# Moving the bias and residual-branch additions of a two-layer metaformer kernel from VectorE to ScalarE and TensorE

## The chip, the cores and the metric

The kernel runs on one core of one Trainium2 chip. The metric is the device time of one execution in microseconds (us), lower is better. An engine is named PE (TensorE, matmuls), DVE (VectorE), ACT (ScalarE), POOL (GpSimd) or SP (SyncE, which only issues transfers here).

## The reference

Input is a batch of 32 images of 96 channels and 48 x 48 pixels. Layer 0 normalises over channels, runs a state-space scan in an order sorted by similarity, adds a local branch (a depthwise convolution, batch normalisation and SiLU), gates and projects the sum, and adds the input back. Then comes a feed-forward layer in emulated low precision. Layer 1 is a 3 x 3 deformable convolution (offsets and masks are predicted from the normalised input, each tap is sampled bilinearly) and a second feed-forward layer. What the change touches, cut down:

```python
out = out_mamba + lc                       # lc: SiLU of the normalised local branch
out = transpose(out) * softmax(z)          # one gate per channel and image
out = out @ out_proj_w.T + out_proj_b      # then x = x + out

def _qlinear(x, W, b):                     # q_mul: 5 exponent, 2 mantissa bits; q_acc: 5 and 10
    y = q_acc(q_mul(x) @ q_mul(W).T)
    return q_acc(y + q_mul(b))
h = relu(_qlinear(_ln_t(t), W1, b1))       # 96 -> 384
t = t + _qlinear(h, W2, b2)                # 384 -> 96
```

## The kernel before

Pass one (from the start to about 10,200 us of the profile) does the scan and leaves the local branch and the scan's result of every image in DRAM. Pass two, which the change touches, does the rest image by image.

Pass two works in periods. An image has NCH = 6 chunks of CH = 384 pixels, and a period handles one chunk of each of several roles at once, for neighbouring images: role c (gate, projection, residual and first feed-forward layer of a chunk), role d (normalisation for layer 1 and the table of corner rows that the sampling reads), role q (offsets and masks), role e (deformable convolution and second feed-forward layer), role f (the second feed-forward layer's last step and the store). A period has 12 steps, numbered u = 0 to 11. In every period the 3 tiles of 128 pixels of role e are sampled: POOL issues 9 indirect gathers for each tile (line 1623, 27 in a period, 162 in an image) into a ring of 4 buffers G, ahead of their use, and may refill a buffer when PE has transposed its tile. DVE multiplies the gathered corners by their weights in `multiply` (lines 1907 to 1912) and adds them in `add_corner` (lines 1925 and 1927), PE transposes the sums (line 1641), ACT copies them to SBUF in `columns` (line 1791).

Each engine runs its instructions strictly in the written order: step by step, and within a step in the order of the code. Semaphores tie the engines together. The order of the work that matters here, for one period, from one deformable convolution to the next:

- u = 3: PE runs the deformable convolution (`convolve`, line 1654, 18 instructions). It waits for ACT's copy of the table rows (`prow`, line 1842).
- u = 3 to 5: first layer normalisation: PE centres (line 1661), ACT squares (1797), PE takes the mean (1668), ACT does Ln (1802) and Exp (1805), DVE multiplies (`xq`, line 1940).
- u = 5 and 6: first linear layer of role c: three matmuls (1678), three copies to 16-bit floats on ACT (`rounded`, line 1812).
- u = 6 and 7: the normalisation of role e in the same manner. At u = 7 DVE adds the bias to the three blocks and takes the positive part (`biased`, line 1948), and ACT turns them to 8-bit floats (`quantized`, line 1819).
- u = 8 and 9: second linear layer (PE, line 1686), copy to 16 bits on ACT (line 1869); DVE adds the second bias (line 1955) and the residual (line 1957, `x_2`). ACT then runs `columns` and the offsets' copy `offc` (line 1852, with a bias).
- u = 10: PE spreads the offsets (line 1756), does the rest of the first linear layer of role e (1678), and centres `x_2` (1661); ACT rounds and squares.
- u = 11: PE takes the mean (1668); DVE runs `biased` for role e; ACT runs `quantized` for role e and then Ln and Exp of the last normalisation, in this order.
- u = 0 (next period): DVE makes `xflat` (line 1975) and adds the local branch to the scan's result (`mix`, line 1980). PE runs the second linear layer of role e (1686), ACT copies it (1832), DVE adds bias and residual at u = 1.
- u = 1 and 2: PE projects (line 1711, one float32 matmul of 384 columns in two instructions) and then transposes `xflat` (line 1721); ACT copies the transposed rows (`prow`, 1842), which frees the next convolution.

Two things happen once in an image. In period 5 (periods of an image are numbered 0 to 5), step 1, and in period 1, step 1, DVE computes sampling positions and weights (`positions`, lines 1550 to 1569). At the end of period 4 ACT applies SiLU to the local branch of the next image but one, between two loads of its function table (line 1881), and DVE's `mix` waits for it.

The 16-bit and 8-bit blocks are `h16`, `r16`, `hq`, `y16`, `z16`; PSUM bank BM takes the projection.

## Time and profile before

| | us |
|---|---|
| runs | 18383.95, 18420.75, 18424.49 |
| median of the runs | 18420.75 |
| span of the profiled execution | 17175.7 |
| median less span | 1245.05 |
| DVE busy in the span | 14514.2 (85%) |
| PE / POOL / ACT busy | 12732.8 (74%) / 12401.2 (72%) / 8968.6 (52%) |

The profile covers the time from the first to the last instruction. The profiled execution's own device time is not listed apart from its span; the three timed runs lie 0.2% from end to end, and what lies around the span is taken as 1245.05 us, the median less the span. Line numbers are those of the kernel before.

### The profile page before, as it was taken

How to read it: one execution, taken by the hardware profiler on the slowest of the kernel's cores; microseconds unless marked ns; L12 is line 12 of the kernel's file. 1: busy time of each engine (PE TensorE's matmuls, PEld its weight loads, DVE VectorE, ACT ScalarE, POOL GpSimd, SP SyncE). 2: the span in 40 equal slices, each digit the busy share in tenths (PEclk: the TensorE clock that was granted, in tenths of full speed). 3: DMA queues.
4: the chain of work that ended last, by engine and by line, in shares of the span. 5: the costliest groups of instructions: out<-in, count | busy, mean ns of one | idle time of the engine just before them, and what ended most of it. 6: DMA issues, size and time to landing. Idle time of an engine off the chain costs nothing. (4 is left out here: it accounts for less than half of the span.)

```text
span 17175.7 us, 183440 instructions
## 1 busy us (share of the span) xinstructions
PE 12732.8 (74%) x51055; PEld 6059.9 (35%) x51055; DVE 14514.2 (85%) x19220; ACT 8968.6 (52%) x16380; POOL 12401.2 (72%) x10756
## 2 busy tenths in 40 slices
PE   6777777777777777777787646777777777777776
PEld 3333333333333333333333312333333333333333
DVE  5888888888888888888888855988898989899998
ACT  4555655656556555565565534444444444444443
POOL 3777777777777777777777744777777777777776
PEclk9999998999999998999999867888888888888887
DMA  2333333333433333333433335666666666666665
GB/s 55 94 97 96 99 100 98 99 95 96 104 94 95 101 98 98 98 98 99 101 97 95 96 90 137 186 187 186 186 188 185 186 192 188 188 188 186 187 188 155
DMA packets 1297936, 2234.90 MB, mean 130 GB/s; under 512 B 713341, under 2 KB 759125, under 8 KB 1284629
## 3 DMA queue, kind: packets, MB, share of 16 engines
q1 hardware_dynamic: 896022, 1090.20, 25.1%
q0 software_dynamic: 368640, 1076.24, 22.3%
q10 hardware_dynamic: 32256, 56.64, 1.1%
q8 instruction: 425, 6.96, 0.2%
q14 instruction: 593, 4.86, 0.1%
HBM read 1493.27 MB, written 275.76 MB: 103 GB/s over the span
## 5 line engine op out<-in xcount | busy, mean ns | idle before, releaser
L1623 POOL DMA_INDIRECT G<-corners,idx x5184 | 4964.2, 958 | 1992.1 <-issue 1554.4
L1383 POOL TENSOR_TENSOR hc<-h,crep 128x768 f32<-128x768 f32 x2304 | 4176.4, 1815 | 2206.5 <-DVE h L1157 1233.9
L1141 DVE TENSOR_TENSOR ps<-dxr,ps 128x768 f32<-128x768 f32 x2304 | 2186.3, 949 | 1041.2 <-PE ps L750 1024.9
L1157 DVE TENSOR_TENSOR_SCAN h<-decay,carry,ps 128x768 f32<-128x768 f32 x1536 | 2776.4, 1808 | 145.5 <-ACT decay L972 85.3
L761 PE MATMUL ps<-hc,sel 128*96 128x512 f32 (+1 forms) x6144 | 2581.8, 548 | 353.4 <-POOL hc L1383 198.7
L972 ACT ACTIVATE decay<-dtr,a_neg 128x768 f32<-128x768 f32 x2304 | 2117.8, 926 | 348.2 <-DVE h L1157 332.8
L750 PE MATMUL ps<-bq,pick 128*128 128x512 bf16 (+1 forms) x4608 | 1233.8, 353 | 991.3 <-DVE h L1157 806.1
L1912 DVE TENSOR_TENSOR G<-G,ps 128x1152 f32<-128x1152 f32 (+1 forms) x1152 | 1724.7, 1497 | 0.0
L761 PEld LDWEIGHTS ps<-hc,sel 128*96 128x96 f32 x6144 | 1022.7, 182 | 1608.1 <-issue 1204.8
L1654 PE MATMUL ps<-cols_t,w_def 128*96 128x384 f32 x3456 | 1342.5, 550 | 178.3 <-ACT prow L1842 172.2
L869 PE MATMUL ps<-xcp,w_local 128*96 128x384 f32 x3456 | 1436.8, 538 | 40.7 <-POOL xcp L1357 39.2
L1925 DVE TENSOR_TENSOR ps<-ps,G 128x384 f32<-128x384 f32 (+1 forms) x2304 | 1407.4, 611 | 47.1
L1157 DVE TENSOR_TENSOR_SCAN h<-decay,ps 128x768 f32<-128x768 f32 x768 | 1342.2, 1748 | 32.3 <-ACT decay L972 2.5
L980 ACT ACTIVATE carry<-h 128x1 f32<-128x1 f32 x1536 | 303.0, 197 | 1934.4 <-DVE h L1157 1932.8
L810 PE MATMUL ps<-xnp,w_conv 128*96 128x384 f32 x3456 | 1292.6, 513 | 24.5 <-ACT x_in L1009 22.3
L1797 ACT ACTIVATE sq<-ps 96x384 f32<-96x384 f32 x576 | 280.1, 486 | 1944.1 <-PE ps L1661 1944.1
L1641 PE MATMUL ps<-ident,G 128*128 128x128 f32 x5184 | 1005.9, 311 | 94.2 <-DVE G L1927 93.1
L750 PEld LDWEIGHTS ps<-bq,pick 128*128 128x128 bf16 x4608 | 377.7, 101 | 1803.2 <-DVE h L1157 923.5
L1791 ACT ACTIVATE cols_t<-ps 128x512 f32<-128x512 f32 (+1 forms) x1728 | 832.8, 483 | 324.2 <-PE ps L1641 323.1
L1641 PEld LDWEIGHTS ps<-ident,G 128*128 128x128 f32 x5184 | 764.0, 162 | 466.6 <-issue 282.9
L1654 PEld LDWEIGHTS ps<-cols_t,w_def 128*96 128x96 f32 x3456 | 626.5, 187 | 831.3 <-issue 598.1
L1686 PE MATMUL ps<-hq,w2q 128*96 128x384 fp8e5 x1152 | 312.0, 389 | 773.8 <-ACT rs L1805 489.4
(243 smaller groups left out, 23803.3 us busy)
## 6 DMA issues: line engine op xcount, KB each, us to landing
crep<-c_rows SPq DMA_DIRECT2D x3072, 96.0 KB
dtr<-rel SPq DMA_DIRECT2D x2304, 96.0 KB, 2.2
dxr<-one_e SPq DMA_DIRECT2D x2304, 96.0 KB
corners<-prow SPq DMA_DIRECT2D x1536, 72.0 KB
G<-corners,idx POOLq DMA_INDIRECT x5184
x_in<-in_x SPq DMA_DIRECT2D x32, 864.0 KB, 6.6
local_all<-local_c ACTq DMA_DIRECT2D x192, 144.0 KB
sim<-sorted_rows SPq DMA_DIRECT2D x32, 864.0 KB, 6.8
```

Of the source, the lines that this page charges most:

```text
L750: m = pe.matmul(wide(bank_of("step", s), P)[:, a:b], Wt["pick"][:, ng, :], M["tall"]["bq"][:, q % 2, a:b], start=True, stop=True)
L761: m = pe.matmul(wide(BY, C)[:, a:b], Wt["sel"][:, cg, :], hc[:, v % HC, a:b], start=(v % ROUND == 0), stop=(v % ROUND == ROUND - 1))
L869: m = pe.matmul(ps[0:C, BV, 0:CH], Wt["w_local"][:, t, :], M["tall"]["xcp"][:, 8 * c + t // 3:8 * c + t // 3 + 8, t % 3:t % 3 + W], start= ...
L972: act.activation(decay[:, s % 3, :], dtr[:, q % 2, cg, :], ACT.Exp, scale=Wt["a_neg"][:, direction(q)[0], ng, cg:cg + 1]).then_inc(S["s_de ...
L1141: dve.tensor_tensor(drive, dxr[:, q % 2, cg, :], drive, ALU.mult).then_inc(S["s_drive"], 1)
L1157: dve.tensor_tensor_scan(along(h[:, v % HR, :], k), along(decay[:, v % 3, :], k), along(wide(bank_of("step", v % STEPS), P), k), first, AL ...
L1383: pool.tensor_tensor(hc[:, v % HC, :], h[:, v % HR, :], crep[:, g % CRING, :], ALU.mult).then_inc(S["s_weighted"], 1)
L1623: pool.indirect_dma_start(M["G"][:, slot(g), k, :], None, table(r), bass.IndirectOffsetOnAxis(M["idx"][side(r)][:, t, k:k + 1], 0)).then_i ...
L1641: m = pe.transpose(ps[:, BT + n % 2, (k % 4) * P:(k % 4 + 1) * P], M["G"][:, slot(t - 1), k, 0:P], ident[:])
L1654: m = pe.matmul(ps[0:C, BN, 0:CH], Wt["w_def"][:, k, :], M["cols"][:, of_e(w)[1] % 2, k, :], start=(k == 0), stop=(k == TAPS - 1))
L1912: dve.tensor_tensor(rows[:, :, 1:], rows[:, :, 1:], by[:, :, 1:].unsqueeze(3).to_broadcast([P, n, CORNERS - 1, C]), ALU.mult).then_inc(S[" ...
L1925: dve.tensor_tensor(acc[:, 0:n], acc[:, 0:n], rows[:, :, q], ALU.add).then_inc(S["p_half"], 1)
```

## The change

Three edits, all in pass two. First, `biased` moves from DVE to ACT: one activation Relu with a per-partition bias for each of the three blocks; the first block is placed at the end of step 6 (role c) or 10 (role e), the other two in step 7 or 11 right ahead of `quantized`. Second, the addition of the second bias moves from DVE to ACT as an Identity activation with a bias, behind the copy of the matmul's result (`returned`); DVE keeps the residual addition. Third, DVE's `mix` is dropped: PE projects the scan's result and the local branch in two matmuls that add up in one PSUM group. SP now loads the next local branch behind the projection (`p_proj`) and no longer behind `mix`. `local_t` gets 128 partitions. Cut to its core:

```diff
--- before.py
+++ after.py
@@ -1422,7 +1422,7 @@
     return dict(
-        tall=tall, x2=[low("x2_0", [L]), low("x2_1", [L])], x_t=low("x_t", [L]), local=b("local_t", [C, L]),
+        tall=tall, x2=[low("x2_0", [L]), low("x2_1", [L])], x_t=low("x_t", [L]), local=low("local_t", [L]),
         mix=low("mix", [L]), wg=low("wg", [C]), xn=low("xn2", [PH, PW]), xflat=b("xflat", [C, CH]),
@@ -1576,10 +1576,8 @@
                     if c is not None:
-                        sp.wait_ge(S["p_mix"], nth(of_c, w) + 1)
+                        sp.wait_ge(S["p_proj"], nth(of_c, w) + 1)
                     sp.dma_start(M["local"][:], dram["local"][image(n)]).then_inc(S["p_local"], 16)
-                    if c is not None:
-                        sp.wait_ge(S["p_proj"], nth(of_c, w) + 1)
                     sp.dma_start(M["mix"][:], dram["mamba"][image(n)]).then_inc(S["p_mamba"], 16)
@@ -1703,13 +1701,16 @@
                 if u == 1 and c is not None:
-                    pe.wait_ge(S["p_mix"], nc_ + 1)
                     if w % NCH == LASTP:
+                        pe.wait_ge(S["p_mamba"], 16 * (next_before(w) + 1))
+                        pe.wait_ge(S["p_silu"], next_before(w) + 1)
                         pe.wait_ge(S["p_gate"], next_before(w) + 1)
...
                         pe.wait_ge(S["p_xn"], nd + 1)
-                    pe.matmul(ps[0:C, BM, 0:CH], M["tall"]["wg"][:], M["tall"]["mix"][:, part(c[1])], start=True,
-                              stop=True).then_inc(S["p_proj"], 1)
+                    for name in ("mix", "local_t"):
+                        m = pe.matmul(ps[0:C, BM, 0:CH], M["tall"]["wg"][:], M["tall"][name][:, part(c[1])],
+                                      start=(name == "mix"), stop=(name == "local_t"))
+                    m.then_inc(S["p_proj"], 1)
                 if u == 1 and d is not None:
@@ -1812,10 +1813,29 @@
 
+            def biased(kind, w, b1, first, last):
+
+                i = turn[kind, w]
+                if first == 0 and turn_before(kind, w):
+                    act.wait_ge(S["p_quant"], NHID * turn_before(kind, w))
+                for j in range(first, last):
+                    act.wait_ge(S["p_rnd"], NHID * i + j + 1)
+                    act.activation(r16[:, KIND[kind], j, :], h16[:, KIND[kind], j, :], ACT.Relu,
+                                   bias=b1[:, j:j + 1]).then_inc(S["p_bias"], 1)
+
+            def returned(n, place, z, b2, done):
+
+                act.wait_ge(S["p_lin" + n], place + 1)
+                act.activation(y16[:, z, :], ps[0:C, BV, 0:CH], ACT.Copy).then_inc(S["p_yr" + n], 1)
+                act.wait_ge(S["p_yr" + n], place + 1)
+                if place:
+                    act.wait_ge(S[done], place)
+                act.activation(z16[:, z, :], y16[:, z, :], ACT.Identity, bias=b2).then_inc(S["p_yb" + n], 1)
+
             def quantized(kind, w):
 
-                act.wait_ge(S["p_bias"], turn[kind, w] + 1)
                 for j in range(NHID):
+                    act.wait_ge(S["p_bias"], NHID * turn[kind, w] + j + 1)
                     act.activation(hq[:, KIND[kind], j, :], r16[:, KIND[kind], j, :], ACT.Copy,
@@ -1828,8 +1848,7 @@
                 if u == 0 and f is not None:
-                    act.wait_ge(S["p_lin3"], nf + 1)
-                    act.activation(y16[:, 1, :], ps[0:C, BV, 0:CH], ACT.Copy).then_inc(S["p_yr3"], 1)
+                    returned("3", nf, 1, Wt["b2q"][1][:], "p_y")
                 if u == 1 and d is not None:
@@ -1847,6 +1866,8 @@
                     rounded("c", w, u - 5)
+                    if u == 6:
+                        biased("c", w, Wt["b1q"][0], 0, 1)
                 if q is not None and u == 9:
@@ -1863,15 +1884,18 @@
                 if u == 7 and c is not None:
+                    biased("c", w, Wt["b1q"][0], 1, NHID)
                     quantized("c", w)
                 if u == 8 and c is not None:
-                    act.wait_ge(S["p_lin1"], nc_ + 1)
-                    act.activation(y16[:, 0, :], ps[0:C, BV, 0:CH], ACT.Copy).then_inc(S["p_yr1"], 1)
+                    returned("1", nc_, 0, Wt["b2q"][0][:], "p_x2")
                 if u in (9, 10) and e is not None:
                     rounded("e", w, u - 9)
+                    if u == 10:
+                        biased("e", w, Wt["b1q"][1], 0, 1)
                 if u == 10 and c is not None:
...
                 if u == 11 and e is not None:
+                    biased("e", w, Wt["b1q"][1], 1, NHID)
                     quantized("e", w)
@@ -1939,21 +1963,9 @@
 
-            def biased(kind, w, b1):
-
-                dve.wait_ge(S["p_rnd"], NHID * (turn[kind, w] + 1))
-                if turn_before(kind, w):
-                    dve.wait_ge(S["p_quant"], NHID * turn_before(kind, w))
-                for j in range(NHID):
-                    m = dve.tensor_scalar(r16[:, KIND[kind], j, :], h16[:, KIND[kind], j, :], b1[:, j:j + 1], 0.0,
-                                          ALU.add, ALU.max)
-                m.then_inc(S["p_bias"], 1)
-
-            def residual(n, c, place, z, b2, res, dst, bsem, done):
-
-                dve.wait_ge(S["p_yr" + n], place + 1)
-                dve.tensor_scalar(z16[:, z, :], y16[:, z, :], b2, None, ALU.add).then_inc(S[bsem], 1)
-                dve.wait_ge(S[bsem], place + 1)
+            def residual(n, c, place, z, res, dst, done):
+
+                dve.wait_ge(S["p_yb" + n], place + 1)
                 dve.tensor_tensor(dst[:, part(c)], res[:, part(c)], z16[:, z, :], ALU.add).then_inc(S[done], 1)
@@ -1973,18 +1985,12 @@
                     dve.tensor_tensor(M["xflat"][:], ps[0:C, BM, 0:CH], M["rs"][:], ALU.mult).then_inc(S["p_xn"], 1)
-                if u == 0 and c is not None:
-                    if p == LASTP:
-                        dve.wait_ge(S["p_silu"], next_before(w) + 1)
-                        dve.wait_ge(S["p_mamba"], 16 * (next_before(w) + 1))
-                    dve.tensor_tensor(M["mix"][:, part(c[1])], M["mix"][:, part(c[1])], M["local"][:, part(c[1])],
-                                      ALU.add).then_inc(S["p_mix"], 1)
                 if p == 1 and u == 1 and has(k):
...
                 if u == 1 and f is not None:
-                    residual("3", f[1], nf, 1, Wt["b2q"][1][:], M["x3"], M["x3"], "p_yb3", "p_y")
+                    residual("3", f[1], nf, 1, M["x3"], M["x3"], "p_y")
                 if u == 2 and c is not None:
@@ -1994,14 +2000,10 @@
                     normalize("1", nc_, BM, M["rs"], M["xq"], "p_xq1", saturate=False)
-                if u == 7 and c is not None:
-                    biased("c", w, Wt["b1q"][0])
                 if u == 8 and e is not None:
...
                 if u == 9 and c is not None:
-                    residual("1", c[1], nc_, 0, Wt["b2q"][0][:], M["x_t"], x2[side(c[0])], "p_yb1", "p_x2")
-                if u == 11 and e is not None:
-                    biased("e", w, Wt["b1q"][1])
+                    residual("1", c[1], nc_, 0, M["x_t"], x2[side(c[0])], "p_x2")
                 if of_tile(t) is not None and sub % 2 == 0:
```

## Rows read from the trace of the kernel before

**Rows 1.** Head of the page: span.
```profile
span 17175.7 us, 183440 instructions
```

**Rows 2.** Stretches: us, then busy us (x) of PE, PEld, DVE, ACT, POOL; clock, DMA, GB/s.
```profile
11370.95:16798.14 5427.19, 3999.02 (x15445) 1984.94 (x15445) 4883.92 (x9127) 2613.97 (x5850) 4033.75 (x4213) 0.81 0.67 187
15358.00:15369.10 11.10, 4.57 (x28) 2.85 (x25) 10.18 (x18) 7.58 (x21) 8.36 (x10) 1.00 0.55 154
15394.60:15406.71 12.11, 7.87 (x22) 4.08 (x22) 11.17 (x21) 6.02 (x14) 9.06 (x11) 0.50 0.69 186
```

**Rows 3.** Groups by line and shape, 12000 to 16000 us.
```profile
L1623 POOL DMA_INDIRECT G<-corners,idx x3104 | 2971.6, 957 | 1028.8 <-issue 931.1 <-PE ps L1641 97.8
...
L1819 ACT ACTIVATE hq<-r 128x384 fp8e5<-128x384 f16 x690 | 308.3, 509 | 251.3 <-DVE r L1948 251.3
...
L1948 DVE TENSOR_SCALAR r<-h,b1q 128x384 f16<-128x384 f16 x690 | 204.2, 350 | 0.0
...
L1711 PE MATMUL ps<-mix,wg 128*96 128x384 f32 x230 | 173.3, 857 | 41.4 <-DVE mix L1980 41.4
...
L1955 DVE TENSOR_SCALAR z<-y,b2q 96x384 f16<-96x384 f16 x230 | 76.8, 334 | 5.2
...
L1852 ACT ACTIVATE offc<-ps,off_bias 96x384 f32<-96x384 f32 x115 | 65.2, 567 | 0.0
...
L1980 DVE TENSOR_TENSOR mix<-mix,local_t 96x384 f32<-96x384 f32 x115 | 62.8, 546 | 56.4 <-ACT local_t L1881 56.4
```

**Rows 4.** Waits, same stretch: who waited for whom, us, times, longest.
```profile
POOL G L1623 <- issue: 931.1, 3056, 0.3
...
ACT hq L1819 <- DVE r L1948: 251.3, 115, 2.9
...
POOL G L1623 <- PE ps L1641: 97.8, 48, 4.9
```

**Rows 5.** Timeline of PE: the deformable convolution of seven periods (start, length).
```profile
15340.68 6.02 PE L1654 MATMUL ps<-cols_t,w_def 128*96 128x384 f32 x18 [0.94 <-ACT prow L1842]
...
15373.67 6.02 PE L1654 MATMUL ps<-cols_t,w_def 128*96 128x384 f32 x18 [0.94 <-ACT prow L1842]
...
15406.71 8.04 PE L1654 MATMUL ps<-cols_t,w_def 128*96 128x384 f32 x18 [0.94 <-ACT prow L1842]
...
15444.18 8.09 PE L1654 MATMUL ps<-cols_t,w_def 128*96 128x384 f32 x18 [0.94 <-ACT prow L1842]
...
15480.75 6.02 PE L1654 MATMUL ps<-cols_t,w_def 128*96 128x384 f32 x18 [0.94 <-ACT prow L1842]
...
15513.64 6.02 PE L1654 MATMUL ps<-cols_t,w_def 128*96 128x384 f32 x18 [0.94 <-ACT prow L1842]
...
15548.94 1.50 PE L1654 MATMUL ps<-cols_t,w_def 128*96 128x384 f32 x4 [0.94 <-ACT prow L1842]
```

**Rows 6.** Timeline of ACT in the first two of those periods.
```profile
15363.50 0.49 ACT L1797 ACTIVATE sq<-ps 96x384 f32<-96x384 f32 x1
15366.71 1.35 ACT L1819 ACTIVATE hq<-r 128x384 fp8e5<-128x384 f16 x3 [2.73 <-DVE r L1948]
...
15389.34 1.33 ACT L1819 ACTIVATE hq<-r 128x384 fp8e5<-128x384 f16 x3
...
15395.90 0.49 ACT L1797 ACTIVATE sq<-ps 96x384 f32<-96x384 f32 x1 [0.73 <-PE ps L1661]
15399.16 1.35 ACT L1819 ACTIVATE hq<-r 128x384 fp8e5<-128x384 f16 x3 [2.77 <-DVE r L1948]
```

**Rows 7.** Timeline of PE in the second of those periods.
```profile
15403.43 1.49 PE L1711 MATMUL ps<-mix,wg 128*96 128x384 f32 x2
15404.71 0.85 PE L1721 MATMUL ps<-ident,xflat 96*96 96x96 f32 x4
```

**Rows 8.** Timeline of DVE: layer 1 normalisation in the second and the fourth period.
```profile
15383.00 0.55 DVE L1940 TENSOR_TENSOR xq<-ps,rs 96x384 fp8e5<-96x384 f32 x1 [1.21 <-ACT rs L1805]
...
15457.88 0.55 DVE L1940 TENSOR_TENSOR xq<-ps,rs 96x384 fp8e5<-96x384 f32 x1
```

2 lines of the change are left out of this document (1 added, 1 removed).

## Prediction

> **What bounds the kernel now.** I read the head of the page first: a span of 17175.7 us [rows 1], so 1245.05 us of the median of 18420.75 lie outside it, and I leave them as they are. The change touches pass two alone, so the next view is the table of stretches over 26 whole images of it [rows 2]: 5427.19 us, or 208.7 us an image and 34.8 a period. DVE is busy for 4883.92 of them (90%), POOL for 74%, ACT for 48%. The reader should distrust both 90% and 74%.
>
> POOL first. In 4000 us it is busy for 2971.6 us and sits for another 931.1 in gaps of 0.3 us with nothing to wait for [rows 3, 4]. So a gather costs 0.957 + 0.300 = 1.257 us of POOL, and the 162 of an image cost 203.7 us. POOL waits for a free buffer for 97.8 us in 19 images, 5.1 us an image [rows 4]. POOL is therefore a floor 5.0 us below today's 208.7, or 33.9 us a period: 32 x 5.0 = 160 us is the most that any relief of the other engines can return.
>
> Then the periods. The timeline of the deformable convolution [rows 5] gives the six intervals of an image, named by the periods at their ends: 2 to 3 32.99, 3 to 4 33.04, 4 to 5 37.47, 5 to 0 36.57, 0 to 1 32.89, 1 to 2 35.30, together 208.26. The convolution takes 6.02 us at the upper level of the clock and 8.04 to 8.09 where it starts at the lower one.
>
> Last, inside a period. ACT waits once in each period for DVE's `biased` of role e, 251.3 us in 115 periods or 2.2 each, and this is its longest wait for DVE [rows 4]; after it come `quantized`, Ln and Exp, the second linear layer, the projection, the transposes, `prow`, and the next convolution. So in a plain period the path goes: convolution, first normalisation, DVE's queue from `xq` to `biased` e, then ACT and PE to the next convolution. DVE's stretch can shrink. The question is what ACT and PE need between the same two points, for that becomes the path.
>
> **What the change removes from DVE.** Per period, from the groups by shape [rows 3]: `biased` 204.2 / 115 = 1.78 us, the two second biases 76.8 / 115 = 0.67, `mix` 62.8 / 115 = 0.55 and its wait for SiLU 56.4 / 115 = 0.49. That is 3.0 us of work and 0.5 of waiting. DVE then needs some 28.3 us of a plain period, and is no longer what decides.
>
> **What it adds to ACT.** No row shows Relu on 16-bit blocks or Identity into them. Nearest: three blocks of `quantized` take 1.33 us in a row, so 0.42 each and 0.49 for one alone [rows 6], and `offc`, with a per-partition bias, takes 567 ns where the square of the same size without one takes 0.49 us [rows 3, 6]. So a bias costs 0.08 us, and I take 0.57 us for a block alone and 0.47 in a row. Bounds: 0.42 (bias free) and 0.60. Eight of them are 3.9 us a period, on an engine busy for half of it; only where they stand matters.
>
> *Role c, step 7.* The first Relu hides in step 6, where ACT waits for PE anyway. The other two stand ahead of `quantized`, right behind Exp: 2 x 0.47 = 0.95 us, on ACT's own path. The second linear layer comes 0.95 later; then the Identity, which must wait for the copy just before it, puts 0.54 between the copy and what follows. So the copy of the next transposed tile, `offc`, the spreading of the offsets, the first linear layer of role e and the centring of `x_2` all start 0.95 + 0.54 = 1.49 later than now. DVE's residual has its operand at about the old time.
>
> *Role e, steps 10 and 11, period 3 to 4* [rows 6]. The square starts at 15395.90 now, so at 15397.39 then, and ends at 15397.88; two Relus (the first was done before the square) bring `quantized` to 15397.88 - 0.05 + 0.95 = 15398.78, where it starts at 15399.16 now. Gain 0.4 us: of the 2.77 us that ACT waited for DVE, nearly all is spent on its own new work and on being 1.49 late.
>
> *The same steps, period 2 to 3.* Here PE ran at full clock (granted 1.00, 2.4 GHz, from 15358 to 15369.1, against 0.50, 1.2 GHz, from 15394.6 to 15406.71 in the other period [rows 2]). The first Relu now stands ahead of the square: 15363.50 + 1.49 + 0.47 = 15365.46. Then square 0.44 and two Relus 0.95 give 15366.85, against 15366.71 now. Loss 0.1 us.
>
> A rule of the Trainium skill speaks for the change here. "Perfetto Trace Analysis", section "Optimizing Scalar/DVE Operations", says that work may pay off on ScalarE once DVE is saturated, and a DVE busy for 90% invites it; by that rule alone DVE's 3.5 us come off every period until the gathers bind, which is the first rival below. "ScalarE: Activation LUTs", "Rules for kernel authors", speaks against it: relu and add belong on VectorE, up to three times as fast per element in 16 bits. The rows agree in direction: 0.30 us a block on DVE, 0.47 to 0.57 on ACT.
>
> **What it adds to PE.** The projection becomes two matmuls of the same size. In step 1 it stands ahead of the transposes of `xflat`, on which `prow` and the next convolution wait. From its start to that of the transposes it is 1.28 us [rows 7], at the lower level; at the upper one, by the convolution's 6.02 / 18 for an instruction, 0.67. All other PE work between Exp and the convolution is unchanged. `mix` did not delay the projection in a plain period, since PE was busy until then. So the second matmul is added in full: 1.28, bound 0.67.
>
> **SP and waits.** SP loads the local branch after the projection of period 4 instead of after `mix`, some 4 us later, and has the whole period of 37 us before SiLU. The load that follows already waited for the projection. Nothing behind it on SP moves. I cost this at nothing; with the cover gone, 4 us an image.
>
> **The sum, an image.** 2 to 3 and 0 to 1: 0.1 + 1.3 = +1.4 each. 3 to 4: -0.4 + 1.3 = +0.9. 4 to 5: SiLU sits on ACT between two table loads, and ACT's queue behind it decides; -0.4 + 0.54 for the Identity = +0.15. 5 to 0: `xq` comes 13.70 us after the convolution's start [rows 5, 8], 9.33 in period 3 with a convolution 2.07 shorter, so DVE (late by SiLU and `positions`) holds it for 2.3 us; that goes, the rest stays: -2.3 + 0.9 to 1.4, I take -1.0. 1 to 2: `positions` holds DVE, 35.30; now it would be 33.0 + 1.2 = 34.2 with the convolution at full clock and 36.2 with it at the lower level; I take 35.1, -0.2. Sum +2.65, times 32 = +85 us.
>
> The clock is the open term. The waits of PE ahead of the second linear layer of role c and ahead of the spreading of the offsets grow by 0.95 and 0.5, so I expect it at the lower level from there on also in intervals like 2 to 3, where it is at the upper one now: the spreading and the centring then take 0.6 each more, of which the Relu hides some 0.5. The longer burst ahead of the convolution works the other way. I take +1.5 us an image, +48. Together +133 on 18420.75: **18550 us**, 0.7% slower.
>
> **Rivals.**
>
> *Faster: the clock stays up and the gathers bind.* At the upper level the PE work from the offsets to `prow`, some 6 us at the lower one in 3 to 4, takes 3 less, and the period falls from 33.9 to 31, under POOL's 33.9. The image then takes POOL's 203.7: -160, 18260 us; part of the way, 18300 to 18380. It decides once a plain period comes under 33.0, that is when some 0.9 to 1.4 of these 3 us come back in most periods. For it: full clock in 2 to 3. Against: PE busy only 4.57 of 11.1 us there, with longer waits to come. 0.15.
>
> *No change.* The relief where SiLU and `positions` hold DVE (2.3 and 1 us) is larger than I take, or the Relus cost 0.42, and the plain periods' loss balances it: 18420. 0.15.
>
> *Slower still.* DVE's queue now hides a slow clock ahead of Exp of role e; when ACT decides, each such delay (the centring and the mean at the lower level, 1.3 to 1.5 us) and each convolution at the lower level (2.0) counts in full. Three of each an image are +10, less what is there already: +5 to +9, 18620 to 18760. 0.15.
>
> **Chances.** My forecast's own case, 18460 to 18640, gets 0.55. Slower by over 0.2% (what a measurement of this kernel can tell from no change): 0.55 + 0.15 = 0.70; within 0.2%: 0.15; faster: 0.15. The range, 18380 to 18700, takes in no change and most of the slower rival, and leaves out the gathers' case.
>
> **What would show it.** In the changed kernel: DVE busy near 80% of pass two (28.3 of 35.4 us), its waits for `xq` (ACT's Exp) grown to 3 or 4 us a period and a new wait for ACT's Identity near 1; no wait of ACT for DVE ahead of `quantized`; the centring of `x_2` some 1.5 us later after the convolution; 2.6 us from the projection's start to the transposes at the lower level; POOL's waits for PE above 5 us an image. Plain intervals of 33.9 to 34.5. If they are near 33 or below, and POOL waits for less, the step that fails is the clock or the place of the second matmul. A table load ahead of Relu would make everything wrong; I know of no reason for one.

## The result, and the profile after

The changed kernel takes 18506.6 us (median of 6 runs, 18487.23 to 18541.14) against 18423.24 us (6 runs) for the kernel before: ratio 1.0051 [1.004, 1.0062], slower by half a per cent. The forecast was 18550 and "slower". The direction and the range hold, but the sum that led there doesn't, and most of this part is about why.

The first thing is the span. Head of the page of the changed kernel:

```profile
span 18525.8 us, 183672 instructions
PE 13198.8 (71%) x50874; PEld 6342.1 (34%) x51439; DVE 14043.7 (76%) x17493; ACT 9780.4 (53%) x17916; POOL 12343.7 (67%) x10756
```

This execution took 18527.84 us by its own time, 2.0 more than its span. So nothing like 1245 us lies around a span: the execution whose profile stands ahead of the prediction [rows 1] was itself shorter than every timed run of the same program, by at least 1206 us against the six above and at least 1088 against those of the experiments (2 us added to its span). In a second profile of the kernel before, first run of the experiments below, the span is 18365.2 us. Pass one is nearly as long in all three (first projection at 10,321.1 us in the first profile of before, 10,303.0 in the second, 10,316.7 in the changed kernel). The difference lies in pass two: (18365.2 - 17175.7) / 192 periods = 6.2 us a period. What the prediction read in detail was a pass two that the timed runs don't have. Stretches from 12000 to 16000 us, first the profile of before that the prediction used, columns as in [rows 2]:

```profile
12000.00:16000.00 4000.00, 2943.22 (x11389) 1460.87 (x11388) 3600.66 (x6724) 1925.84 (x4312) 2971.20 (x3104) 0.81 0.67 187
```

the kernel before in its second profile:

```profile
12000.00:16000.00 4000.00, 2744.57 (x9672) 1354.74 (x9672) 3063.02 (x5710) 1653.09 (x3669) 2511.67 (x2639) 0.73 0.56 159
```

and the changed kernel:

```profile
12000.00:16000.00 4000.00, 2750.54 (x9684) 1366.23 (x9684) 2767.25 (x4750) 2013.69 (x4367) 2450.31 (x2590) 0.73 0.55 156
```

DVE is busy for 90% in the first, 77% in the second, 69% in the third. The second and third are the pair to compare. POOL's gathers (3104, 2639, 2590) count the progress: 1.9% fewer after the change, in a stretch.

Groups of the changed kernel that answer to [rows 3]:

```profile
L1621 POOL DMA_INDIRECT G<-corners,idx x2590 | 2451.3, 946 | 1550.0 <-issue 704.2 <-PE ps L1639 607.8 <-remote 237.9
L1823 ACT ACTIVATE r<-h,b1q 128x384 f16<-128x384 f16 x576 | 330.0, 604 | 0.0
L1711 PE MATMUL ps<-mix,wg 128*96 128x384 f32 x192 | 142.0, 843 | 25.6 <-issue 25.6
L1711 PE MATMUL ps<-local_t,wg 128*96 128x384 f32 x192 | 124.7, 747 | 0.0
L1833 ACT ACTIVATE z<-y,b2q 96x384 f16<-96x384 f16 x192 | 118.1, 615 | 6.2
L1964 DVE TENSOR_TENSOR xq<-ps,rs 96x384 fp8e5<-96x384 f32 x192 | 106.2, 553 | 641.6 <-ACT rs L1806 390.6 <-issue 251.0
L1969 DVE TENSOR_TENSOR x<-x_t,z 96x384 f32<-96x384 f32 x96 | 53.3, 555 | 314.7 <-ACT z L1833 281.2 <-issue 33.5
```

The same groups in the second profile of the kernel before, and one more that matters below, ACT's copy of the second linear layer of role c:

```profile
L1623 POOL DMA_INDIRECT G<-corners,idx x2639 | 2512.1, 952 | 1492.1 <-issue 715.0 <-PE ps L1641 495.8 <-DMA mamba_all<-rest 281.4
L1819 ACT ACTIVATE hq<-r 128x384 fp8e5<-128x384 f16 x588 | 262.5, 509 | 68.4 <-DVE r L1948 52.9 <-issue 15.3
L1948 DVE TENSOR_SCALAR r<-h,b1q 128x384 f16<-128x384 f16 x588 | 167.8, 340 | 17.4 <-ACT h L1812 13.7 <-issue 3.7
L1955 DVE TENSOR_SCALAR z<-y,b2q 96x384 f16<-96x384 f16 x196 | 67.7, 346 | 299.7 <-ACT y L1869 260.9 <-issue 38.5
L1980 DVE TENSOR_TENSOR mix<-mix,local_t 96x384 f32<-96x384 f32 x98 | 53.5, 546 | 47.5 <-ACT local_t L1881 44.5 <-issue 3.0
L1869 ACT ACTIVATE y<-ps 96x384 f16<-96x384 f32 x98 | 47.6, 486 | 337.0 <-remote 327.2 <-PE ps L1686 6.9 <-issue 2.8
```

The reader should see three things. The removed work is what was reckoned: 167.8 + 67.7 + 53.5 = 289.0 us in 98 periods, 2.95 a period (predicted 3.0). But ACT's wait for DVE ahead of `quantized`, 251.3 us in [rows 4] and the very thing that the change relieves, is only 52.9 us here. And ACT waits 337.0 us, 3.4 a period, ahead of its copy `y`, 327.2 of them for a releaser that the profile can't name ("remote").

The first profile differs from all thirteen later ones in one more thing. Counted in the packed traces from 12000 to 16000 us, it holds 696 recorded semaphore updates for each period (27 gathers), the others 219 to 287, though the kernel before gives the same number of them each time. In pass one (4000 to 8000 us) the counts are 71,433 and some 65,000. So most updates of pass two left no record in the later profiles, and some long waits there have a wrong name or none (in e1_before 607.0 us of ACT's waits ahead of its squares are put down to "issue"). The figures below rest on the starts and ends of instructions, not on those records.

### The profile page after: what moved, and what is told of

Same layout as the page of the kernel before. It is cut to its first block and busy times, and to the rows that moved or that the text cites. A ratio compares the mean times of both kernels' runs of the same rounds, so it can differ in the third digit from the quotient of the medians.

```text
span 18525.8 us, 183672 instructions
## 1 busy us (share of the span) xinstructions
PE 13198.8 (71%) x50874; PEld 6342.1 (34%) x51439; DVE 14043.7 (76%) x17493; ACT 9780.4 (53%) x17916; POOL 12343.7 (67%) x10756
## 5 line engine op out<-in xcount | busy, mean ns | idle before, releaser
L1621 POOL DMA_INDIRECT G<-corners,idx x5184 | 4906.3, 946 | 3391.8 <-issue 1420.9
L750 PE MATMUL ps<-bq,pick 128*128 128x256 bf16 (+1 forms) x4043 | 1091.5, 342 | 1090.2 <-DVE h L1157 850.0
L1652 PE MATMUL ps<-cols_t,w_def 128*96 128x384 f32 x3456 | 1229.2, 513 | 232.2 <-ACT prow L1861 191.7
L1964 DVE TENSOR_TENSOR xq<-ps,rs 96x384 fp8e5<-96x384 f32 x384 | 212.5, 553 | 1253.3 <-ACT rs L1806 782.3
L1639 PE MATMUL ps<-ident,G 128*128 128x128 f32 x5184 | 1088.8, 332 | 72.9 <-ACT cols_t L1792 35.1
L1639 PEld LDWEIGHTS ps<-ident,G 128*128 128x128 f32 x5184 | 853.8, 177 | 510.4 <-issue 420.3
L1666 PE MATMUL ps<-sq,mean 128*96 128x384 f32 x1152 | 697.3, 697 | 343.1 <-ACT sq L1798 223.1
```

Source lines behind the costliest of these rows:

```text
L750: m = pe.matmul(wide(bank_of("step", s), P)[:, a:b], Wt["pick"][:, ng, :], M["tall"]["bq"][:, q % 2, a:b], start=True, stop=True)
L1621: pool.indirect_dma_start(M["G"][:, slot(g), k, :], None, table(r), bass.IndirectOffsetOnAxis(M["idx"][side(r)][:, t, k:k + 1], 0)).then_i ...
L1639: m = pe.transpose(ps[:, BT + n % 2, (k % 4) * P:(k % 4 + 1) * P], M["G"][:, slot(t - 1), k, 0:P], ident[:])
L1652: m = pe.matmul(ps[0:C, BN, 0:CH], Wt["w_def"][:, k, :], M["cols"][:, of_e(w)[1] % 2, k, :], start=(k == 0), stop=(k == TAPS - 1))
```

## Where the time is in an image

Seven convolutions of one image in the changed kernel (timeline of PE) answer to [rows 5]; here the starts of periods 4, 5, 0 and 1:

```profile
13385.40 6.02 PE L1652 MATMUL ps<-cols_t,w_def 128*96 128x384 f32 x18 [0.94 <-ACT prow L1861]
13434.77 8.21 PE L1652 MATMUL ps<-cols_t,w_def 128*96 128x384 f32 x18 [0.94 <-ACT prow L1861]
13475.77 6.02 PE L1652 MATMUL ps<-cols_t,w_def 128*96 128x384 f32 x18 [1.26 <-ACT prow L1861]
13516.14 6.02 PE L1652 MATMUL ps<-cols_t,w_def 128*96 128x384 f32 x18 [0.94 <-ACT prow L1861]
```

49.37 us from period 4 to 5, then 41.00 and 40.37. The kernel before in its second profile, one image, the same four periods less the last, and period 3 ahead of them:

```profile
12310.37 6.02 PE L1654 MATMUL ps<-cols_t,w_def 128*96 128x384 f32 x18 [1.12 <-ACT prow L1842]
12349.91 7.71 PE L1654 MATMUL ps<-cols_t,w_def 128*96 128x384 f32 x18 [2.29 <-ACT prow L1842]
12391.83 7.45 PE L1654 MATMUL ps<-cols_t,w_def 128*96 128x384 f32 x18 [0.94 <-ACT prow L1842]
12434.18 6.02 PE L1654 MATMUL ps<-cols_t,w_def 128*96 128x384 f32 x18 [1.73 <-ACT prow L1842]
```

39.54, 41.92, 42.35. The table takes the differences of such starts over 29 images of each profile, and the share of all convolutions that take 6.02 us (the upper level of the clock). Names of runs are those of the experiments.

| kernel (profile) | 2-3 | 3-4 | 4-5 | 5-0 | 0-1 | 1-2 | mean | at 6.02 |
|---|---|---|---|---|---|---|---|---|
| before, first profile | 33.03 | 33.78 | 36.70 | 36.96 | 33.05 | 35.31 | 34.81 | 0.47 |
| before (e1_before) | 39.91 | 40.60 | 42.14 | 42.22 | 40.04 | 41.17 | 41.01 | 0.30 |
| biases on ACT alone (e1_biases) | 40.05 | 40.25 | 42.94 | 41.54 | 40.23 | 41.12 | 41.02 | 0.26 |
| two-matmul projection alone (e1_projection) | 39.75 | 39.93 | 43.60 | 40.80 | 40.15 | 40.61 | 40.81 | 0.76 |
| changed kernel (after) | 40.70 | 40.64 | 45.88 | 41.70 | 40.19 | 41.35 | 41.74 | 0.81 |
| changed, repeated (e1_after) | 40.94 | 40.78 | 46.51 | 41.10 | 40.09 | 41.06 | 41.74 | 0.80 |
| additions narrowed (e2_light) | 40.54 | 40.94 | 42.02 | 42.19 | 39.68 | 40.91 | 41.05 | 0.18 |
| before, refill in thirds (e2_release) | 45.22 | 45.18 | 44.04 | 42.78 | 44.68 | 44.15 | 44.34 | 0.08 |
| changed, refill in thirds (e2_release_after) | 42.76 | 43.19 | 42.97 | 42.49 | 43.39 | 42.52 | 42.89 | 0.35 |
| changed, SiLU in step 5 (e2_silu_after) | 41.03 | 40.21 | 45.49 | 41.34 | 40.86 | 41.04 | 41.66 | 0.85 |
| before, loads together (e3_together_before) | 39.59 | 40.23 | 41.53 | 41.85 | 39.71 | 40.40 | 40.55 | 0.28 |
| changed, loads apart (e3_spread_after) | 40.67 | 41.25 | 42.54 | 40.58 | 40.72 | 41.59 | 41.23 | 0.82 |
| projection alone, loads apart (e3_spread_projection) | 39.78 | 40.67 | 42.13 | 40.43 | 39.65 | 39.93 | 40.43 | 0.71 |
| before, pauses on POOL (e3_pause) | 39.93 | 41.56 | 40.81 | 41.71 | 41.52 | 40.77 | 41.05 | 0.03 |

The last four rows are from another group of runs, in which the kernel before ran 0.5% faster (18302.5 against 18403 and 18416 us), 0.5 us a period if all of it lies in pass two. The table is of single executions: the spans of the two compared most, after and e1_before, lie 161 us apart, the medians of the result 83. Of the 4.4 us an image that the changed kernel loses to e1_before, 3.7 lie in the interval 4 to 5. The plain intervals (2 to 3, 3 to 4, 0 to 1) grow by 0.8, 0.0 and 0.2, not by the 1.4, 0.9 and 1.4 of the forecast.

What happens in the interval 4 to 5 is seen in the timeline of the changed kernel, all engines, from 12 us behind the convolution of 13385.40:

```profile
13396.86 0.60 DVE L1959 SCALAR_TENSOR_TENSOR x<-ps,cols,x 96x384 f32<-96x384 f32 x1
...
13397.52 0.89 PE L1659 MATMUL ps<-x,centring 128*96 128x384 f32 x2 [0.15 <-issue]
13397.53 0.95 POOL L1621 DMA_INDIRECT G<-corners,idx  x1 [0.30 <-issue]
...
13406.29 0.95 POOL L1621 DMA_INDIRECT G<-corners,idx  x1 [0.30 <-issue]
13410.20 0.49 ACT L1798 ACTIVATE sq<-ps 96x384 f32<-96x384 f32 x1 [9.59 <-remote]
13410.74 1.59 PE L1666 MATMUL ps<-sq,mean 128*96 128x384 f32 x2 [11.55 <-ACT sq L1798]
```

PE centres the input of role e's normalisation at 13397.52 and is done at 13398.41; ACT's square, which needs nothing else, starts at 13410.20. The increment of the semaphore that PE gives with the matmul is recorded at 13410.17. POOL issues gathers all the while, one each 1.25 us, and the square comes 2.96 us behind the end of the last. Taken for 26 images (start of the square less the modelled end of the centring, in period 4), the time is 0.6 us on average in e1_before, 0.3 in e1_biases, 3.1 in e1_projection, 4.8 in the changed kernel and 7.5 in its repetition. In the first profile of before it is 0.04 us, on average over 158 periods of all kinds. The images of one profile bear out what it costs. In the changed kernel 18 of 29 squares of period 4 came over 1 us late, and there the interval 4 to 5 takes 47.9 us; in the other 11 it takes 42.5. In e1_before 3 of 29 came late (44.7 us, the others 41.9). So of the 3.7 us that the changed kernel loses from 4 to 5, some 3.1 go with the late squares (5.4 x 18/29 less 2.8 x 3/29) and some 0.6 are there without them.

It has another place in every period, here in the second profile of the kernel before:

```profile
12049.71 0.66 PE L1686 MATMUL ps<-hq,w2q 128*96 128x384 fp8e5 x3 [1.34 <-ACT hq L1819]
...
12051.63 0.95 POOL L1623 DMA_INDIRECT G<-corners,idx  x1 [0.30 <-issue]
12053.03 0.49 ACT L1869 ACTIVATE y<-ps 96x384 f16<-96x384 f32 x1 [2.99 <-remote]
...
12054.79 0.94 POOL L1623 DMA_INDIRECT G<-corners,idx  x1 [2.21 <-DMA mamba_all<-rest]
```

PE's second linear layer is done at 12050.37 and ACT gets it 2.66 us later, behind POOL's last gather of the tile; POOL's own release, by a transposition that ended at 12051.07, comes at 12054.5. The waits that answer to [rows 4], second profile of the kernel before (the loads named in the second line are not what POOL waits for; in the timeline above it is that transposition):

```profile
POOL G L1623 <- PE ps L1641: 495.8, 164, 10.4
POOL G L1623 <- DMA mamba_all<-rest: 281.4, 128, 2.3
ACT y L1869 <- remote: 327.2, 87, 5.3
```

and the same wait in the first profile of before, where it was 0.4 us at most:

```profile
ACT y L1869 <- PE ps L1686: 41.4, 115, 0.4
```

and in the changed kernel:

```profile
POOL G L1621 <- PE ps L1639: 607.8, 176, 11.5
ACT y L1829 <- remote: 130.8, 48, 3.8
ACT y L1829 <- PE ps L1684: 63.7, 63, 2.0
```

## The experiments

**1. The kernel before, once more (e1_before).** No edit.

> The kernel before, unchanged, for a second profile: the first one had a span of 17175.7 us while the runs take 18420, the changed kernel's span of 18525.8 is 2 us under its own run's time. Theory A (the 1245 us lie outside the span, as the prediction took it): span again near 17176 and period of pass two 34.7 us. Theory B (the profiled execution was a faster one than the timed ones, with the same program): a profile with a span near 18420 and a period near 41 us, with waits that the first profile does not show.

Measured: 18398.58 us, ratio 0.9998 [0.9989, 1.0007], span 18365.2. The short span of [rows 1] does not come back (theory B).

**2. Both biases on ACT, `mix` and the single matmul kept (e1_biases).** On the kernel before, the hunks of the change on `biased`, `returned`, `quantized` and `residual`; their core:

```diff
-                m = dve.tensor_scalar(r16[:, KIND[kind], j, :], h16[:, KIND[kind], j, :], b1[:, j:j + 1], 0.0,
...
+                    act.activation(r16[:, KIND[kind], j, :], h16[:, KIND[kind], j, :], ACT.Relu,
...
-                dve.tensor_scalar(z16[:, z, :], y16[:, z, :], b2, None, ALU.add).then_inc(S[bsem], 1)
...
+                act.activation(z16[:, z, :], y16[:, z, :], ACT.Identity, bias=b2).then_inc(S["p_yb" + n], 1)
```

> Both biases on ACT, mix still an addition on DVE and one projection matmul. Path theory (ACT and PE set the period after the change, the second matmul adds 1.28 us to it, 192 times): 245 us under the changed kernel, so about 18260, clearly faster than before (0.991). DVE-relief theory (only DVE's load matters): as the changed kernel or slower, since 0.5 us a period is back on DVE, 18500 to 18600.

Measured: 18425.03 us, ratio 1.0016 [1.0007, 1.0025]. Neither theory: no gain down to 18260, and 75 us or more short of 18500 to 18600.

**3. The projection by two matmuls, biases kept on DVE (e1_projection).** The other hunks, those on SP's loads too; their core:

```diff
-                    pe.matmul(ps[0:C, BM, 0:CH], M["tall"]["wg"][:], M["tall"]["mix"][:, part(c[1])], start=True,
-                              stop=True).then_inc(S["p_proj"], 1)
+                    for name in ("mix", "local_t"):
+                        m = pe.matmul(ps[0:C, BM, 0:CH], M["tall"]["wg"][:], M["tall"][name][:, part(c[1])],
+                                      start=(name == "mix"), stop=(name == "local_t"))
+                    m.then_inc(S["p_proj"], 1)
```

> The projection in two matmuls, both biases still on DVE. Path theory: DVE still sets the stretch up to biased of role e, 0.5 us less of it, and 1.28 us more behind: +0.8 us a period, +150 us, 18570. If the second matmul is hidden: -0.5 us a period, 18320.

Measured: 18402.59 us, ratio 1.0002 [0.9993, 1.0011]. Neither 18570 nor 18320. The interval 4 to 5 grows by 1.5 us and 5 to 0 falls by 1.4.

**4. The changed kernel again, beside the parts (e1_after).** No edit.

> The changed kernel again, on the chip of the other three, for a second profile: 18507 expected (1.005 of before). If its profile shows a period of 34 to 36 us in place of 41.6, the two regimes belong to executions and not to kernels.

Measured: 18583.85 us, ratio 1.0098 [1.0084, 1.0113]. The period of 41.74 us is that of the first profile of the changed kernel. The parts together cost more than their sum, 0.5 to 1.0% against 0.2%. Not all of the 1.0% need be pass two: in the profiled executions the first projection starts at 10,363.5 us here and at 10,303.0 in e1_before, so 60 of the 217 us between these two spans lie ahead of it.

**5. POOL's wait in thirds, on the kernel before (e2_release).**

```diff
-                if g - GRING >= -1 and of_tile(g - GRING) is not None:
-                    pool.wait_ge(S["p_tturn"], 3 * (turned_before(g - GRING + 1) + 1))
+                ring = g - GRING >= -1 and of_tile(g - GRING) is not None
                 for k in range(TAPS):
+                    if ring and k % 4 == 0:
+                        pool.wait_ge(S["p_tturn"], 3 * turned_before(g - GRING + 1) + k // 4 + 1)
```

> The kernel before, with one edit: POOL waits for the freeing of a ring buffer in three parts (taps 0 to 3 once the first third of the tile is transposed, 4 to 7 after the second, tap 8 after the last) instead of once for all nine taps. The wait that is looked at is POOL's at the head of each tile, 2.6 us on average in the traces with periods of 40.8 us (18.6 us an image of 245). Theory A, POOL's queue of gathers sets the period and that wait is the part of it that can go: 27 x 1.257 = 33.9 us of POOL a period, plus three waits of some 2 us, are the 39.4 us seen in every plain period; with the wait released two steps (some 6 us) earlier plain periods fall to 34 to 36 us and the time to 17200 to 17600 us. Theory B, the 39.4 us come from the drain of the gathers' transfers or from DVE's queue, and POOL only waits for what is late anyway: the wait moves to another tap or gathers land later, plain periods stay at 39.4 and the time within 0.5% of 18403.

Measured: 18972.91 us, ratio 1.0298 [1.0268, 1.0327]. Neither theory: POOL let go on earlier makes the kernel 3% slower. The waits of its profile, 12000 to 16000 us:

```profile
ACT sq L1798 <- PE ps L1662: 964.1, 231, 10.0
DVE xq L1941 <- ACT rs L1806: 728.7, 129, 14.2
POOL G L1624 <- PE ps L1642: 714.5, 111, 10.1
ACT cols_t L1792 <- DMA mamba_all<-rest: 620.1, 164, 11.3
PE ps L1655 <- ACT prow L1843: 547.1, 68, 13.4
```

With all releasers taken together, and against e1_before: POOL stops for a buffer 11.5 us a period instead of 8.0, DVE waits 8.8 instead of 4.0 for `xq`, ACT 8.3 instead of 3.8 for `columns`, PE 8.0 instead of 1.7 for the convolution. ACT's wait for its squares is about the same (11.6 and 11.2), and the square of role e in period 4 comes late in none of the images here.

**6. The same edit on the changed kernel (e2_release_after).**

> The changed kernel with the same edit of POOL's wait in three parts. In the changed kernel the interval from period 4 to period 5 is 45.9 us against 42.1 in the kernel before; there the third part of a tile's transposes stands on PE behind the projection, which waits for SiLU and has one more matmul, and POOL stops for 5.1 us. Theory A (that stop sets the interval): with eight of nine taps released before the projection the interval falls by 2 to 4 us and the changed kernel loses no more to the kernel before with the same edit than 0.2%, or gains on it. Theory B (the interval is set by ACT's and PE's own chain through SiLU, projection, transposes and prow to the convolution): the interval stays 3 to 4 us longer than in the kernel before with the same edit, and the difference of the two is again 0.5 to 1%.

Measured: 18832.74 us, ratio 1.0243 [1.0214, 1.0272]. The interval 4 to 5 falls from 45.9 to 43.0 and the other five grow by 0.8 to 3.2 us. Against run 5 the changed kernel is the faster, 18832.74 / 18972.91 = 0.993 (four runs each, and the ranges just touch: 18728 to 18914 and 18911 to 19022). So the sign of the change can turn with when POOL is let go on.

**7. SiLU in step 5 instead of step 11, on the changed kernel (e2_silu_after).**

```diff
-                if w % NCH == LASTP - 1 and u == 11 and next_one(w) is not None:
+                if w % NCH == LASTP - 1 and u == 5 and next_one(w) is not None:
```

> The changed kernel with SiLU and its two table loads (4.9 us of ACT) moved from step 11 to step 5 of the same period, so that the projection of period 5 never waits for SiLU. Theory A (the extra time of the changed kernel sits where SiLU, the double projection and the Identity stand behind one another): the interval from period 4 to 5 falls from 45.9 us to 40 to 42, 4 to 5 us an image or 130 to 160 us in all: 18350 to 18450, at or below the kernel before. Theory B (the loss is spread over all periods by the Relus and the second matmul, as the prediction had it): 4 to 5 falls but 3 to 4 grows by as much, and the time stays at 18500 to 18580.

Measured: 18536.25 us, ratio 1.0062 [1.0045, 1.0078]; 4 to 5 is 45.49 us. The loss isn't the wait for SiLU at the end of the period; but SiLU in step 5 itself holds ACT for 4.9 us of the same interval, so that the run doesn't say what SiLU costs.

**8. DVE relieved on the kernel before (e2_light).** The additions of the corners take 24 channels of 96, in all three of their instructions; the rest of the sampled sum is left out.

```diff
-                    dve.tensor_tensor(acc[:, 0:n], acc[:, 0:n], rows[:, :, q], ALU.add).then_inc(S["p_half"], 1)
+                    dve.tensor_tensor(acc[:, 0:n, 0:24], acc[:, 0:n, 0:24], rows[:, :, q, 0:24], ALU.add).then_inc(S["p_half"], 1)
```

> The kernel before with DVE's additions of the gathered corners narrowed from 96 to 24 channels (part of the sampling is left out; the number of instructions and all waits stay). This takes some 6 to 8 us of DVE's work out of each period, twice what the change takes out. Theory A (POOL's gathers and their waits set the plain period of 39.4 us, DVE has slack): the period stays at or above 39.4 us and the time falls by no more than 32 x 6 x 1.4 = 270 us, to 18130 or more. Theory B (DVE's queue sets the period, as the prediction took from the profile of before): the period falls by 4 to 7 us to POOL's 33.9 to 36, the time to 17300 or less.

Measured: 18376.94 us, ratio 0.9979 [0.9969, 0.9989]. The instruction falls from 662 to 288 ns at five taps (groups of its profile) and from 560 to 260 at four:

```profile
L1925 DVE TENSOR_TENSOR ps<-ps,G 128x120 f32<-128x120 f32 x584 | 168.0, 288 | 13.4
```

DVE's busy time of 4000 us falls from 3063.0 to 2476.5, 6.0 us a period, twice what the change takes out, and the kernel gains 0.2%. DVE does not set the period.

**9. Both loads of period 4 issued together, on the kernel before (e3_together_before)** (as the changed kernel does).

```diff
                         sp.wait_ge(S["p_mix"], nth(of_c, w) + 1)
+                        sp.wait_ge(S["p_proj"], nth(of_c, w) + 1)
                     sp.dma_start(M["local"][:], dram["local"][image(n)]).then_inc(S["p_local"], 16)
-                    if c is not None:
-                        sp.wait_ge(S["p_proj"], nth(of_c, w) + 1)
```

> The kernel before with one edit on SP: the load of the next local branch waits for the projection as well, so that both 864 KB loads of period 4 are issued together, as in the changed kernel. In the traces so far the gathers' transfers pause twice for 3.0 to 3.5 us behind these loads in the kernel before and once for 6.6 to 8.1 us in the changed kernel. Theory A (the bunched loads are a good part of what the changed kernel loses from period 4 to 5): the gathers' pause is one of 6 to 8 us, the interval 4 to 5 grows from 42.1 to 43.5 us or more, the time by 32 x 1.5 to 4 us, 50 to 130 us: 18450 to 18530. Theory B (the change of the loads costs nothing, as the prediction had it): time within 0.1% of the kernel before.

Measured: 18319.91 us against 18302.52, ratio 1.0003 [0.9994, 1.0012]. The gathers' transfers do pause longer around the convolution of period 4, 6.4 us between two starts in the middle one of 29 images, where e1_before has 3.0 and the changed kernel 7.2, and it costs nothing in the kernel before.

**10. The loads apart, on the changed kernel (e3_spread_after).** The local branch is loaded behind the table stores.

```diff
                     sp.wait_ge(S["p_store"], stored)
+                if w % NCH == LASTP - 1 and n is not None:
+                    sp.dma_start(M["local"][:], dram["local"][image(n)]).then_inc(S["p_local"], 16)
```

> The changed kernel with the load of the next local branch issued behind the table stores of period 4, some 12 us after the other load, still 15 us or more ahead of SiLU. Theory A (bunched loads starve the gathers and hold back increments of PE): two pauses of 3 to 4 us, the long waits of ACT for the centring of role e in period 4 (4.8 us on average, up to 12) mostly go, the interval 4 to 5 falls from 45.9 to 42 to 43.5 us and the time by 80 to 130 us, to 18400 to 18440. Theory B (those waits come from where the faster convolution puts the centring against POOL's gathers, whatever the loads do): the interval stays above 45 us and the time at 18500 to 18560.

Measured: 18458.22 us, ratio 1.0075 [1.0061, 1.0089]. The interval 4 to 5 does fall, to 42.5 us, and the late square of period 4 from 4.8 to 0.4 us. But late squares now turn up in periods 0, 1 and 3 (1.2, 2.1 and 1.4 us on average), and the total is no better. The lateness moves; it isn't removed. The changed kernel as it is has no run in this group, so 1.0075 stands only beside its 1.0051 and 1.0098 of the other two.

**11. The same edit on the projection alone (e3_spread_projection).**

> Only the third edit of the change (projection of both branches by two matmuls), with the local load issued behind the table stores. With the loads together this part ran in 18402.6 us, ratio 1.0002: 1.4 us lost from period 4 to 5 and 1.4 gained from 5 to 0. Theory A: with the loads apart the loss of 4 to 5 goes and the gain stays, 32 x 1.0 to 1.5 = 30 to 50 us: 18350 to 18375, faster than the kernel before by 0.2 to 0.3%. Theory B: 4 to 5 is longer by the second matmul itself, and the time stays at 18400.

Measured: 18336.51 us, ratio 1.0013 [1.0004, 1.0023]. The hoped-for version faster than both kernels isn't there: 4 to 5 loses less, and the time is no lower.

**12. Pauses on POOL, on the kernel before (e3_pause).** A memset of 128 x 512 behind the third and the sixth gather of each tile.

```diff
                                             ).then_inc(S[f"p_got{slot(g)}"], 16)
+                    if k in (2, 5):
+                        if paused[0]:
+                            pool.wait_ge(S["p_idle"], paused[0])
+                        pool.memset(M["idle"][:], 0.0).then_inc(S["p_idle"], 1)
+                        paused[0] += 1
```

> The kernel before with a small memset on POOL behind the third and the sixth gather of each tile (six a period, 0.3 to 0.6 us each, 2 to 3.5 us of POOL a period). In the traces of 40.8 us a period POOL stops for 2.6 us at the head of each tile, and increments of PE arrive only once it has stopped. Theory A (an unbroken run of gathers holds the increments back, and short breaks let them through): the stop at the tile head falls by more than the memsets take and plain periods fall below 39.4 us. Theory B (the stop at the head is there because a buffer is not free, and POOL has slack of that size): the stop shrinks by just what the memsets take, plain periods stay at 39.4, the time within 0.3%. Theory C (POOL's own issue and those stops add up to the 39.4 us, without slack): plain periods grow by the memsets' 2 to 3.5 us, the time by 400 to 650 us, to 18800 to 19050.

Measured: 18424.69 us, ratio 1.0055 [1.0037, 1.0073]. Groups of its profile:

```profile
L1625 POOL DMA_INDIRECT G<-corners,idx x2628 | 2521.3, 959 | 1164.1 <-issue 683.1 <-PE ps L1648 360.2 <-DMA mamba_all<-rest 120.8
L1631 POOL MEMSET idle<- 128x512 f32 x584 | 317.2, 543 | 0.2
```

Six memsets of 0.543 us are 3.3 us a period, 625 us in 192 periods; 0.55% of 18302.52, 101 us of them, are seen (the medians are 122 apart). POOL's stops for a buffer fell from 495.8 + 281.4 to 360.2 + 120.8 us, 3.0 a period. So POOL has slack too, most of what was added: the result lies between theory B (nothing) and C (all of it), much nearer to B, and what the remaining sixth is the run doesn't explain.

## Why the prediction was right, and where it wasn't

**The span.** The step "1245.05 us of the median of 18420.75 lie outside it, and I leave them as they are" failed, and with it the whole picture of pass two. Runs put 2 us there. A gap of 7% between a profiled span and every timed run was the sign that this profile was not of such a run.

**What bounds pass two.** "DVE's queue from `xq` to `biased` e" failed for the timed runs: ACT's wait there is 52.9 us in 98 periods against 251.3 in 115, and 6.0 us less of DVE a period are worth 0.2% (run 8). The other half, POOL's floor, failed too: plain periods of about 40 us (39.9, 40.6 and 40.0 in e1_before) stand far above 33.9, and POOL bears most of 3.3 us more (run 12). "The most that any relief of the other engines can return" was worked out from gathers that POOL issues, and that isn't what ends last.

**The work moved.** DVE's 2.95 us a period (3.0 predicted). A Relu block is 604 ns alone (0.57), and two in a row start 0.51 apart (0.47); the Identity 0.615 (0.54). Against DVE's 340 and 346 ns, a block costs 1.8 times as much on ACT. The direction of the Trainium skill's "ScalarE: Activation LUTs", "Rules for kernel authors" (relu and add on VectorE, up to about three times as fast there in bf16) is what these rows show, for fp16, and with 1.8. But neither engine's cost decided anything: alone, the biases cost 0.16%.

**The centring of `x_2` "1.49 later than now".** The first link held: in period 2 to 3 `quantized` of role c starts 20.95 us behind the convolution instead of 19.69 (averages over 27 images, as are the next ones). The last didn't: the centring comes at 29.09 instead of 28.99. Between them stands ACT's late copy `y`, at 24.55 instead of 24.60. Its wait absorbs the Relus: 337.0 us in 98 periods, and 130.8 + 63.7 in 96 after. DVE's wait for the Identity is 281.2 / 96 = 2.9 us a period, not near 1, for the same reason.

**The second matmul "added in full".** From the projection's start to the transposes of `xflat`, 2.56 us in the period shown (2.6 predicted), at the lower level of the clock:

```profile
13258.42 1.49 PE L1711 MATMUL ps<-mix,wg 128*96 128x384 f32 x2
13259.70 1.49 PE L1711 MATMUL ps<-local_t,wg 128*96 128x384 f32 x2
13260.98 0.85 PE L1722 MATMUL ps<-ident,xflat 96*96 96x96 f32 x4
```

The size was right, the step wrong: alone, the edit costs nothing (run 3). In period 2 to 3 `prow` starts 2.2 us after the transposes in e1_before and 1.2 in the changed kernel, and from the projection's start to the convolution's it is 4.07 us in e1_before, 4.38 with the second matmul alone and 4.31 in the changed kernel, not 1.28 more. That a late increment ahead of `prow` takes up the new work is the likely reading, as it does for `y`; in the first profile of before, `prow` started 1.28 us after the transposes.

**The clock.** "I expect it at the lower level" failed for the convolution: it takes 6.02 us in 0.81 of the periods after the change, in 0.30 before, in 0.76 with the second matmul alone and in 0.26 with the biases alone. The busier stretch ahead of it "works the other way", as the text allowed, and stronger. What that gives, 1 to 2 us earlier at the centring of role e in period 4 (its end 13.98 us behind the convolution instead of 15.71), is where the late increments are found: of the squares whose centring ended between 13.0 and 14.5 us, 22 of 27 came late in the changed kernel, of the other 131 that ended later only 2. In e1_before only three ended that early, and these three alone came late.

The rival "Slower still" has a slip: +5 to +9 us an image, times 32, give 18580 to 18710, not 18620 to 18760.

**SP costed at nothing** held (run 9). **The interval 4 to 5**, costed at +0.15 us, is +3.7, the largest term of all and the one that was mis-sized. The sum had no late increment in it, some 3.1 of the 3.7, and gave this interval no second matmul, though the projection behind SiLU has it too; without a late square the interval grew by 0.6. Of the once-an-image terms, 5 to 0 fell by 0.5 (-1.0 forecast) and 1 to 2 grew by 0.2 (-0.2 forecast). Together the forecast's +133 us and the measured +83 (+181 in run 4) agree by luck: the sum put them into plain periods and the clock, and they lie for the most part in one interval of six.

**Signs it named.** POOL's waits for PE did go above 5 us an image (607.8 / 16 = 38). DVE is busy for 69%, not near 80, its wait for `xq` is 641.6 / 96 = 6.7 us a period, not 3 or 4, and plain intervals are 40 to 41 us, not 33.9 to 34.5.

**What stays open.** Why increments of PE reach ACT and POOL 2 to 12 us late while POOL issues gathers, and why one execution of the kernel before was free of it. Shown is that the lateness is there in every profile but that one (from 12000 to 16000 us, 21 to 90 of ACT's waits ahead of `y` end over 1 us behind the modelled end of PE's second linear layer, and none of 211 in the first profile of before), that it ends behind POOL's last gather in the two timelines, that waits grow where POOL is let go on earlier (5), and that it moves to other places when the work is shifted (6, 10). That POOL's issue causes it is argued, not shown; a kernel with fewer gathers wasn't tried. Another rival is untested too: that the recording itself takes part. The one execution without late increments is the one that recorded 696 semaphore updates a period against 219 to 287, and the runs of the experiments all have a recorded span and clock, so none of them shows the kernel unrecorded. The two facts go together; which of them brings the other, if either does, is not shown. The 40 us of a plain period are not explained either: neither DVE (8) nor POOL's own work (12) nor the loads (9) sets them.

## What to carry to other kernels

Hold the span of a profile against the timed runs, and what it recorded against other profiles, before you read a row of it; if they differ by more than a few us, the stage that differs isn't the one you are asked about. Busy time moved from one engine to another pays only if the receiving wait ends last in the runs that count: take twice the work away from the engine in question, and see. Where waits end on a releaser that the profile can't name, work added ahead of them may be free, and work made faster ahead of them may gain nothing.

## What was not expected of the hardware

- A semaphore increment given with a matmul arrived up to 12 us behind the matmul's modelled end (13398.41 to 13410.17), with nothing else for ACT to do, and the square followed it at once.
- Letting the gathers start earlier made the kernel 3% slower (run 5), and 3.3 us of idle work on POOL in each period cost 0.5 us (run 12).
- One execution of the kernel before had a pass two of 34.8 us a period, another 41.0, and all timed runs were as long as the other; with the DMA at 187 against 159 GB/s and the same mean time for a transfer of one size (0.281 and 0.276 us for 4608 bytes). The short one recorded 696 semaphore updates a period, the long one 243.
